# Decoder layer on one core: earlier output blocks in the last expert pass, accumulation moved ahead of the low part, a split copy and filler matmuls

## The reference

```
x = layernorm(x + linear_attention(rms_norm(x)) )   # q,k,v = silu(W x), g = sigmoid(Wg x), causal in each sequence
x = layernorm(x + cross_attention(x, ctx) )          # 16 heads, rope, softmax over 64 context rows, low-rank weights
x = layernorm(x + experts(x))                        # 32 experts of 96 hidden units, top 8, softmax routing
expert e:  acc += (silu(x Wg_e) * (x Wu_e)) Wd_e * combine[:, e]
```

## Time and profile before

| | |
|---|---|
| time, median of 3 runs | 893.08 us (892.21 to 893.61) |
| the profiled execution: its own time | 894.03 us |
| the profiled execution: span from first to last instruction | 892.1 us |
| PE busy | 849.6 us, 95% of the span |
| DVE busy | 629.9 us, 71% |
| ACT busy | 280.2 us, 31% |
| POOL busy | 143.6 us, 16% |
| mean granted clock of PE, share of full speed | 0.989 |

### The profile page before, as it was taken

How to read it: one execution, slowest core, us unless ns; L and a number is a source line. 1 busy time by engine, 2 the same in 40 slices (tenths; PEclk the granted TensorE clock), 3 DMA queues, 4 the chain that set the end, 5 groups by cost and what they waited for, 6 DMA issues and landing times.

```text
span 892.1 us, 14708 instructions
## 1 busy us (share of the span) xinstructions
PE 849.6 (95%) x5720; PEld 668.3 (75%) x5720; DVE 629.9 (71%) x1379; ACT 280.2 (31%) x502; POOL 143.6 (16%) x122
## 2 busy tenths in 40 slices
PE   8999999998999989999799989999999999999994
PEld 6966677776777768777477878788888888888873
DVE  3566787888878888779687765766565666566647
ACT  5431243212422034211443522333322333233232
POOL 2024301333013330134340400300000000000021
PEclk9999999999999999999899999999999999999997
DMA  9310000100001000000230014110212020000001
GB/s 331 125 37 1 1 2 1 48 1 18 1 1 48 7 11 1 1 24 4 85 103 1 25 38 145 44 55 2 87 48 65 0 88 29 29 1 1 1 24 71
DMA packets 12685, 35.82 MB, mean 40 GB/s; under 512 B 1488, under 2 KB 2384, under 8 KB 12112
## 3 DMA queue, kind: packets, MB, share of 16 engines
q1 hardware_dynamic: 12624, 34.98, 11.4%
HBM read 30.33 MB, written 2.36 MB: 37 GB/s over the span
## 4 chain that ended last, share of the span: by engine, by line
PE 81%; DVE 11%; issue 4%; ACT 2%; POOL 1%; DMA 0%; ACTq 0%; DVEq 0%; POOLq 0%
PE ps L246 20%; PE ps L247 19%; PE ps L248 19%; PE ps L1419 6%; PE ps L1499 5%; PE ps L1490 2%; PE ps L1293 2%; PE ps L1475 1%; PE ps L1329 1%; DVE small L1095 1%; DVE h_lo L348 1%; DVE su L511 1%; DVE xT_lo L960 1%; PE ps L1358 1%; PE ps L1286 1%
## 5 line engine op out<-in xcount | busy, mean ns | idle before, releaser
L511 DVE TENSOR_TENSOR su<-sg,ps 128x512 f32<-128x512 f32 x96 | 66.0, 687 | 132.8 <-PE ps L248 131.6
L246 PE MATMUL ps<-y_hi,f_hi 128*128 128x512 f32 x384 | 151.1, 394 | 0.0
L248 PE MATMUL ps<-y_hi,f_lo 128*128 128x512 f32 x384 | 149.5, 389 | 0.0
L247 PE MATMUL ps<-y_lo,f_hi 128*128 128x512 f32 x384 | 149.4, 389 | 0.0
L375 ACT ACTIVATE sg<-ps 128x512 f32<-128x512 f32 x96 | 57.3, 598 | 258.1 <-PE ps L248 258.1
L739 POOL TENSOR_TENSOR roped<-prod 128x512 f32<-128x512 f32 x64 | 80.9, 1285 | 170.2 <-DVE prod L1040 170.2
L1040 DVE TENSOR_TENSOR prod<-ps,ropeq 128x512 f32<-128x512 f32 x128 | 79.4, 682 | 27.1 <-PE ps L248 26.5
L246 PEld LDWEIGHTS ps<-y_hi,f_hi 128*128 128x128 f32 x384 | 72.2, 188 | 15.3 <-issue 0.5
L247 PEld LDWEIGHTS ps<-y_lo,f_hi 128*128 128x128 f32 x384 | 72.2, 188 | 15.3 <-issue 0.5
L248 PEld LDWEIGHTS ps<-y_hi,f_lo 128*128 128x128 f32 x384 | 72.1, 188 | 15.1
L246 PE MATMUL ps<-xT_hi,a_hi 128*128 128x512 f32 x192 | 78.4, 408 | 3.7 <-DVE xT_lo L960 3.7
(11 more groups left out here) (160 smaller groups left out, 1328.7 us busy)
## 6 DMA issues: line engine op xcount, KB each, us to landing
cb<-routing SPq DMA_DIRECT2D x32, 256.0 KB
f_raw<-in_L_ffn_gate_up_proj SPq DMA_DIRECT2D x8, 768.0 KB, 6.1
f_raw<-in_L_ffn_down_proj SPq DMA_DIRECT2D x8, 384.0 KB, 7.0
xb<-in_x SPq DMA_DIRECT2D x4, 512.0 KB, 4.6
lq<-in_L_xattn_Wq SPq DMA_DIRECT2D x1, 2048.0 KB, 16.2
x2T_all<-in_L_xattn_Wo SPq DMA_DIRECT2D x1, 2048.0 KB, 12.1
x2T_all<-x2T SPq DMA_DIRECT2D x4, 512.0 KB, 3.3
out<-res SPq DMA_DIRECT2D x4, 512.0 KB, 2.6
```

The costliest lines, as they stand in the source:

```text
L246: pe.matmul(dst, l_hi, r_hi, start=first, stop=False, skip_group_check=check)
L247: pe.matmul(dst, l_hi, r_lo, start=False, stop=False, skip_group_check=check)
L248: return pe.matmul(dst, l_lo, r_hi, start=False, stop=last, skip_group_check=check)
L511: dve.tensor_tensor(su[:, k % 2], sg[:, k % 2], bank(2 * (k % 2) + 1), ALU.mult).then_inc(s_su, 1)
```

## The change

It has four parts.

1. **Fold.** The copies of `m_w` are shared: ACT copies the upper 64 partitions (four copies), DVE the lower 64 (four copies, after its second silu). PE waits for both.
2. **Last cross attention.** Matmuls on a tile of ones are put between others: 6 after `scores(0)`, 3 after `scores(2)`, 2 after `scores(3)`. Each is 128x256 in plain float32. Nobody reads what they write.
3. **Accumulation**, in all passes: it stands in DVE's steps 4, 7, 10 and so on (1, 4, 7 ... in the later passes), behind `hc(k)` and ahead of `h_lo(k-1)`.
4. **Last pass.** The order of the sets is (0,0) (0,1) (0,2) (1,0) (1,1) (1,2) (0,3) (1,3), so that blocks 0 to 2 are complete after steps 11, 14 and 17. Their `turn_out` stands in steps 15, 18 and 21, their statistics in DVE's steps 15, 18 and 22, their scale in 16, 19 and behind step 23, `final_apply` in 17, 20 and behind the loop. The second group's f_hi is made in steps 2 to 4 (before 4 to 6), its f_lo in steps 3 to 8 (before 5 to 10). POOL makes h_lo in steps 14 to 21 (before 17 to 23), DVE the last two. The last accumulation is done in two halves of 256 tokens, and PE starts its transposes after the first. The last block is stored by two transfers in place of one.

```diff
...
@@ -268,13 +267,15 @@
-    def turn_of(nb, first):
-
-        return FIRST_ORDER[nb] if first else (nb // BLOCKS % 2, nb % BLOCKS)
-
-    def place(k, first):
-
-        return (*turn_of(k // ROWS, first), k % ROWS)
+    LAST_ORDER = ((0, 0), (0, 1), (0, 2), (1, 0), (1, 1), (1, 2), (0, 3), (1, 3))
+
+    def turn_of(nb, first, last=False):
+
+        return FIRST_ORDER[nb] if first else LAST_ORDER[nb] if last else (nb // BLOCKS % 2, nb % BLOCKS)
+
+    def place(k, first, last=False):
+
+        return (*turn_of(k // ROWS, first, last), k % ROWS)
@@ -327,8 +328,8 @@
-    f_hi_step = lambda w, first: (20 if first else 14) if w == 0 else 4
-    f_lo_step = lambda w: 15 if w == 0 else 5
+    f_hi_step = lambda w, first, last: (20 if first else 14) if w == 0 else 2 if last else 4
+    f_lo_step = lambda w, last: 15 if w == 0 else 3 if last else 5
@@ -343,16 +344,16 @@
-        if eng is nc.gpsimd and k == POOL_STEP:
+        if eng is nc.gpsimd and k == POOL_STEPS[0]:
             eng.wait_ge(s_hlo, done)
         eng.tensor_tensor(h_lo[:, k % 3], hc[:, k % 2], h_hi[:, k % 3].bitcast(F32), ALU.subtract).then_inc(s_hlo, 1)
 
     X2_STEPS, LOGITS_STEP, ROUTE_STEPS, TURN_C = (2, 4), 5, (8, 8, 9, 9, 10, 10), 11
     NORM2_STEP = 1
 
-    FINAL_BANKS = (4, 4, 0, 2)
-    POOL_STEP = 17
-    FINAL_STEP = 18
+    FINAL_BANKS = (4, 4, 4, 0)
+    POOL_STEPS = range(14, 22)
+    TURN_OUT_STEPS, STATS_STEPS, SCALE_STEPS, APPLY_STEPS = (15, 18, 21), (15, 18, 22), (16, 19, 23), (17, 20)
@@ -386,21 +387,21 @@
-                if 4 <= k < 7:
-                    if k == 4:
+                part = k - f_hi_step(1, first, last)
+                if 0 <= part < 3:
+                    if part == 0:
                         act.wait_ge(s_fload[1], it * 32 + 32)
-                    f_hi_out(act, 1, k - 4)
-                part = k - f_hi_step(0, first)
+                    f_hi_out(act, 1, part)
+                part = k - f_hi_step(0, first, last)
                 if 0 <= part < 3 and not last:
                     if part == 0:
                         act.wait_ge(s_fload[0], it * 32 + 64)
                         act.wait_ge(s_d, base + (6 if first else 4) * ROWS)
                     f_hi_out(act, 0, part)
-                if last and k == FINAL_STEP + 3:
-                    final_apply(0)
+                if last and k in APPLY_STEPS:
+                    final_apply(APPLY_STEPS.index(k))
             if last:
                 hi(STEPS - 1)
-                final_apply(1)
...
@@ -460,11 +461,15 @@
-            sp.wait_ge(s_res, TILES * (n + 1) - 2 * (n == LAST))
             if n == LAST:
                 sp.wait_ge(s_res_end, 2)
-            sp.dma_start(out[n], res[:, n]).then_inc(s_out, 16)
-        sp.wait_ge(s_out, 16 * BLOCKS)
+                sp.dma_start(out[n, :, 2:4], res[:, n, 2:4]).then_inc(s_out, 16)
+                sp.wait_ge(s_res, TILES * n + 2)
+                sp.dma_start(out[n, :, 0:2], res[:, n, 0:2]).then_inc(s_out, 16)
+            else:
+                sp.wait_ge(s_res, TILES * (n + 1))
+                sp.dma_start(out[n], res[:, n]).then_inc(s_out, 16)
+        sp.wait_ge(s_out, 16 * (BLOCKS + 1))
...
@@ -495,30 +500,36 @@
-                w, n = turn_of(nb, first)
+                w, n = turn_of(nb, first, last)
                 if first and w == 0 and n == LAST:
                     dve.wait_ge(s_kept, 32 * LAST + 17)
                 dve.wait_ge(s_d, base + ROWS * (nb + 1))
                 dve.wait_ge(s_acc, it * NB + nb + 1)
-                dve.tensor_tensor(acc[:, :, cols(n)], acc[:, :, cols(n)], ps[:, 6:8, :], ALU.add).then_inc(s_acc, 1)
+                halves = 2 if last and nb == NB - 1 else 1
+                for i in range(halves):
+                    s = slice(i * BT // halves, (i + 1) * BT // halves)
+                    a = acc[:, :, n * BT + s.start:n * BT + s.stop]
+                    dve.tensor_tensor(a, a, ps[:, 6:8, s], ALU.add).then_inc(s_acc, 1)
 
             for k in range(STEPS):
-                if (k - 5) % ROWS == 0 and (not first or k >= 5):
-                    accumulate((k - 5) // ROWS)
-                w, n, j = place(k, first)
+                w, n, j = place(k, first, last)
                 dve.wait_ge(s_sg, base + k + 1)
                 dve.wait_ge(s_up, base + k + 1)
                 dve.tensor_tensor(su[:, k % 2], sg[:, k % 2], bank(2 * (k % 2) + 1), ALU.mult).then_inc(s_su, 1)
                 if j == 0:
                     dve.wait_ge(s_cb[w][n], it * 16 + 16)
-                if last and k >= POOL_STEP + 2:
+                if last and k - 2 in POOL_STEPS:
                     dve.wait_ge(s_hlo, base + k - 1)
                 dve.wait_ge(s_su, base + k + 1)
                 dve.tensor_tensor(hc[:, k % 2], su[:, k % 2], cb[:, w, cols(n)], ALU.mult).then_inc(s_hc, 1)
-                if (not first or k >= 1) and not (last and k > POOL_STEP):
+                if (k - 4) % ROWS == 0 and (not first or k >= 4):
+                    accumulate((k - 4) // ROWS)
+                if last and k == POOL_STEPS[-1] + 2:
+                    dve.wait_ge(s_hlo, base + k - 1)
+                if (not first or k >= 1) and not (last and k - 1 in POOL_STEPS):
                     lo(k - 1)
                 for w, g in ((1, 2 * it + 1), (0, 2 * it + 2)):
-                    part = k - f_lo_step(w)
+                    part = k - f_lo_step(w, last)
@@ -530,15 +541,14 @@
-                if last and k in (FINAL_STEP + 1, FINAL_STEP + 2):
-                    final_norm(0, k - FINAL_STEP - 1)
-                if last and k == FINAL_STEP + 4:
-                    final_norm(1, 0)
+                if last and k in STATS_STEPS:
+                    final_norm(STATS_STEPS.index(k), 0)
+                if last and k in SCALE_STEPS[0:2]:
+                    final_norm(SCALE_STEPS.index(k), 1)
             if last:
-                final_norm(1, 1)
-                final_norm(2, 0)
+                lo(STEPS - 1)
+                final_norm(2, 1)
                 accumulate(NB - 1)
-                final_norm(2, 1)
...
@@ -587,22 +597,25 @@
-                pe.wait_ge(s_acc, GROUPS * BLOCKS - BLOCKS + n + 2)
-                if n == 1:
-                    pe.wait_ge(s_res, TILES)
-                if n >= 2:
-                    pe.wait_ge(s_su, GROUPS * BLOCKS * ROWS + n - LAST)
+                pe.wait_ge(s_acc, it * NB + LAST_ORDER.index((1, n)) + 2)
+                if n in (1, 2):
+                    pe.wait_ge(s_res, TILES * n)
+                if n == LAST:
+                    pe.wait_ge(s_su, base + STEPS - 1)
                 f = FINAL_BANKS[n]
                 for t in range(TILES):
+                    if n == LAST and t == 2:
+                        pe.wait_ge(s_acc, it * NB + NB + 2)
                     for m in range(KC):
                         c = n * BT + t * P
                         mm = pe.transpose(ps[:, f + t // 2, (t % 2) * D + m * P:(t % 2) * D + (m + 1) * P],
                                           acc[:, m, c:c + P], ident[:])
-                mm.then_inc(s_ft, 1)
+                    if t == TILES - 1 or n == LAST and t == 1:
+                        mm.then_inc(s_ft, 1)
 
             for k in range(STEPS):
                 if not first or k >= 2:
-                    ffn_up(pe, it, k, first)
+                    ffn_up(pe, it, k, first, last)
@@ -613,13 +626,10 @@
-                if last and k == FINAL_STEP:
-                    turn_out(0)
-                if last and k == FINAL_STEP + 3:
-                    turn_out(1)
+                if last and k in TURN_OUT_STEPS:
+                    turn_out(TURN_OUT_STEPS.index(k))
             if last:
                 dn(STEPS - 2)
-                turn_out(2)
@@ -805,10 +815,8 @@
-                for h in range(2):
-                    act.activation(m_w[64 * h:64 * h + 64, 2 * g:2 * g + 2, :],
-                                   ps[64 * h:64 * h + 64, m_bank(g, h), :].rearrange("p (r n) -> p r n", r=2),
-                                   ACT.Copy).then_inc(s_m, 1)
+                act.activation(m_w[0:64, 2 * g:2 * g + 2, :],
+                               ps[0:64, m_bank(g, 0), :].rearrange("p (r n) -> p r n", r=2), ACT.Copy).then_inc(s_m, 1)
@@ -1009,7 +1017,14 @@
-            for i in range(6):
+            silu(b, 0)
+            silu(b, 1)
+            for g in range(PAIRS // 2):
+                dve.wait_ge(s_mps, g + 1)
+                dve.tensor_scalar(m_w[64:P, 2 * g:2 * g + 2, :],
+                                  ps[64:P, m_bank(g, 1), :].rearrange("p (r n) -> p r n", r=2), 1.0, None, ALU.mult)\
+                    .then_inc(s_m2, 1)
+            for i in range(2, 6):
...
@@ -1557,14 +1574,17 @@
+                keep_warm(6, 3)
                 scores(1)
                 turn(0)
                 context(0)
                 scores(2)
+                keep_warm(3, 7)
                 turn(1)
                 project(0)
                 context(1)
                 scores(3)
```

(1 more changed line is left out.)

23 lines of the change are left out of this document (12 added, 11 removed).

## The result

The changed kernel takes 886.12 us, median of 4 runs (885.96 to 886.25), against 892.64 (891.67 to 893.61) for the kernel before in 4 runs: ratio 0.9927, 95% interval 0.9915 to 0.9939. The forecast was 885.8. The profiled execution took 886.25, with a span of 884.4 and a mean clock of 0.995 (before: 894.03, 892.1 and 0.989).

The account below looks back on a forecast made before the run. PE's products bound the full passes, so gain lay in PE's waits and the tail. Terms -0.27, -0.45, -3.2, -0.8, +1.55, -0.8, -3.5, +0.2 sum to -7.3: median 885.8 us, range 884.3 to 887.2.

Parts of the forecast that it names:

- The bound: Middle passes: PE's products bound them, so nothing can be gained there; all gain comes from PE's waits and the tail.
- Fold: Fold: sharing copies between ACT and DVE leaves 0.1 of PE's 0.37 us wait; -0.27 us (0 to -0.45).
- Last cross attention: Last cross attention: matmuls on ones fill PE's 2.98 us wait and turn(0)'s half takes 0.66 for 1.12; -0.45 us.
- if the clock stays up: Last cross attention: condition for the -0.45 us; 0 if the clock falls all the same.
- First pass: First pass, accumulation ahead of h_lo: -3.2 us at step 10, with about 0.9 wait before turn_c; -0.8 at step 22.
- f_lo: Last pass, step 9: PE newly waits 1.49 us for the sixth f_lo part, plus 0.08 for the first matmul; +1.55 us.
- Rival 1: Step 9 or before turn_c: the clock falls in a new wait, costing 1.2 to 1.5 us; 887.2 us, chance 0.12.
- The end: Last pass: -0.8 us from step 9 to ffn_up(23)'s end, then -3.5 in the tail, 16.05 becoming 12.5.
- rival 2: Last pass: scale chains of steps 16 and 19 held by POOL, or turn_outs wait for final_apply; 887 to 889, chance 0.13.
- Store: Behind the last result: two stores in place of one, the second issued about 0.4 later; +0.2 us (0 to 0.45).
- From the sum to the median: Whole kernel: profile 894.03 becomes 886.7; it lay 0.95 above the median of 893.08, so the median becomes 885.8.
- Rivals 3 and 4: 3: routing before turn_c keeps 2.4 us, 891.1, chance 0.06. 4: h_lo late in every set, 901 at 1.1 late, 0.02.

Follow-up runs that it names:

- the experiment: Last pass's odd-weight ACT copies and DVE f_lo parts made one step earlier, against the changed kernel: 884.48 us, 1.64 less.
- the old end: Last pass put back as before the change, the rest as in the changed kernel: median 888.43 us, 2.3 more than the changed kernel.
- two doses: Changed kernel with extra DVE work before 16 middle-pass h_los: 128x1024 each took 899.86 us, half of it 891.48 us.

## Why the prediction was right, point by point

**The bound.** That all gain lies where PE waits held: the middle passes are 98.00 of 98.00 before and after. That they can only lose was 0.2 us off: they lost nothing and gained 0.18.

**Fold.** Direction right, term too small: -0.46 for -0.27. I priced the one wait in brackets. The row of the second pair of groups was 2.38 us long before and is 2.08 now, so another 0.3 of waiting was hidden inside a row of 64 matmuls. Of the 0.37 in brackets 0.21 stays, more than the 0.1 that I took: DVE begins its copies at 16.25, behind its second silu, and each takes 0.69, the upper bound that I gave.

**Last cross attention.** The mechanism is right (turn(0) at 0.66, DVE 0.45 earlier) and the size is off: -0.29 for -0.45. What failed is the condition "if the clock stays up": the sign that I named, full clock from 438 to 445, is not in this profile, and with the clock down the calls of three and two no longer "fall where PE waits for DVE anyway". In the three profiles in which the clock did stay up the term is 29.09 - 28.63 = 0.46 us, as predicted. Whether the clock stays up I could not have known from one profile.

**First pass.** -3.2 and -0.8 predicted, -3.3 (with a small wait near 508) and -0.84 measured. The wait before turn_c stands with 0.65 in its bracket, 0.81 with the overlap of 0.16, for 0.9. What I did not know is that about half of these 3.2 us, 1.6 by the profiles and 1.7 by the runs, is there only in the runs in which the clock falls.

**f_lo.** +1.55 predicted, 1.56 between the two profiles and 1.64 by the experiment; the clock did not fall behind it. Rival 1 did not happen.

**The end.** In the loop -0.8 was predicted and -0.57 measured. The three turn_outs stand where I put them and PE waits for none; their price was too low. Each takes 0.79 us until the next ffn_up starts, and this one then lasts 2.84 (835.49 to 838.33) in place of 2.72: 0.9 and not 0.8, three times. The tail, counted as the prediction counts it, from 0.23 behind the start of the last matmul, was 12.58 for 12.5. The scale chains of steps 16 and 19 were held as described, one small step each for 1.29 and 1.28 us, to the end of POOL's h_lo (842.44 + 1.28 = 843.72; DVE's 842.45 + 1.29 = 843.74). PE waited for none of it: rival 2 did not happen. The Trainium skill, SBUF — State Buffer, section Who interferes with whom, says that a DVE instruction with two SBUF inputs contends with a GpSimd instruction that reads SBUF, and that one with at most one SBUF input does not, outside DVE's two-port modes (an exception that the prediction left out, and that no run here tests). The trace agrees on both sides: beside a POOL h_lo that ran from 838.36 to 839.65, su (one input in PSUM) took 0.69 at 838.60, and beside POOL's f_lo parts (567.08 to 569.51) the accumulation took 1.21 at 568.56, both as elsewhere, while hc, with both inputs in SBUF, took 1.57 at 848.42 beside a POOL h_lo from 848.17, for 0.69.

**Store.** +0.2 predicted, nothing measured. The two halves of the last block go out at 881.32 and 881.69, and the span ends 3.1 us behind the last result, as it did with one transfer.

**From the sum to the median.** This step was wrong by itself, and that 885.8 came so close to 886.12 is in part luck. The pieces give -7.7 and not -7.3, which would be 886.3 for the profiled execution; it took 886.25, and I had 886.7. I then took off 0.95, as the profile before lay so far above the median of its runs. The profile after lies 0.13 above its median. So the terms left the forecast 0.45 us too high, this step took it 0.8 too low, and together they are 0.3 off. The 0.95 hangs on the clock: runs of the kernel before lie between mean clocks of 0.987 and 0.993, and in its profile the clock is low for about 7 us in the last cross attention and for about 3 behind dn(9); after the change it is low for about 3 and not at all. So the medians differ by 6.5 us and the two profiles by 7.8.

Rivals 3 and 4 are excluded: the routing leaves 0.65 us before turn_c and not 2.4, the old end costs its 3.4 us of tail, and h_lo has 0.5 us to spare.

## What to carry to other kernels

Price a new or removed wait on PE by landmarks and not by its bracket: two of 1.33 and 0.56 were worth 1.6 and 0.86 us. Before a kernel's pipeline order is changed, measure the spare of the step that gets something put ahead of it by giving it a known extra piece of work; two doses gave the same 0.5 us here. Matmuls that only hold the clock gave nothing here where DVE's chain ended last, and cost 0.17 us where they stood before a transpose that DVE had already released. And before a step of an argument is called wrong by one profile, look for other profiles of the same program: nine of them spread from 28.62 to 30.07 us here.
